# First attention group's norm, transposes, query and key moved into the last two steps of the text layers

## The chip, the cores and the metric

The kernel runs on one core of a Trainium2 chip. The metric is the device time of one execution in microseconds (us); the time of a kernel is the median over its runs. The engines are TensorE (PE), VectorE (DVE), ScalarE (ACT), GpSimd (POOL) and the DMA queues, of which SyncE (SP) issues most.

## What is computed

The model joins an image and a text, runs one attention layer over both and one layer of experts. Cut to what matters:

```python
h = concat([tokens_of_patches(x), text(x_txt)], axis=1)   # 32 sequences of 37 + 77 = 114 rows of 256
h = h + attention(layernorm(h))
h = h + experts(layernorm(h))

def text(tokens):                     # four layers
    xp = x @ W_in.T;  x_in, gate = split(xp)
    u = silu(causal_conv4(x_in) + cb)
    hs = scan(u @ WB.T)               # h = 0.95 h + 0.05 bu along the sequence
    y = (hs @ WC.T + Dv * u) * silu(gate)
    x = layernorm(y @ Wo.T + x) * g + b

def attention(x):
    qk = silu(x @ wqk + bqk);  q = qk*gamma0 + beta0;  k = qk*gamma1 + beta1
    v = silu(x @ wv + bv)
    a = causal(0.5*(1 + erf(...(q @ k.T / S + rel_bias))))
    return a @ v
```

The experts are eight, of which each row goes to two: the rows are scattered to tables by expert, and 64 blocks of 128 rows are worked through.

## The kernel before

The program has five instruction streams, one per engine, each written out by hand; semaphores alone order the engines among each other, and each engine works strictly in the order of its own stream. That order is the subject here.

**Text layers.** The 32 sequences stand in 8 groups of 4 (308 columns). A text step is one group of one layer, so there are 32 steps, 0 to 31 (`STEPS` is 32). They are pipelined: in iteration i the functions `text_step(i, a, b, o, t)` of the engines work on steps a = i, b = i-1, o = i-2 and t = i-3, and a part whose step does not exist is left out. Iterations 32, 33 and 34 therefore only drain steps 29 to 31. Step 31 ends so: PE multiplies `u` by W_B (L1241, L1249), DVE scans it (`scan`, L1689), ACT takes the upper half of the scanned state (`upper_state`, L773) and DVE the lower (`lower_state`, L1694), PE multiplies by W_C (`state_out`, L1261 and L1262, four chunks), DVE adds and gates (`skip` L1675, `gated` L1683), ACT and POOL split y into two halves (`upper_half` L766, `lower_half` L1026), PE adds the residual (L1273) and multiplies by W_out (L1278), DVE and POOL normalise (`row_stats`, `row_scale` L1019 and L1021, `row_norm` L1723), and POOL applies gain and shift (`keep_gain` L1050, `keep_rows` L1058). POOL's `text_step` runs one iteration ahead of the others in its numbering: its `lower_half(b, ...)` of iteration 31 waits for what ACT does in iterations 32 and 33.

**Between text and attention.** When the rows of a group are kept, SP stores them to memory (L617). After each pair of groups it waits for the stores and loads finished sequences, image and text rows together, into `h_all` (L625), group by group, `ld_h` counting them. The first four groups are loaded during the text layers, the last four after the last store.

**Attention.** 8 groups again, pipelined over 13 iterations of `attn_step(i)` on each engine. For a group g the parts are, in the order of their dependence:

- `norm_ahead_stats` (DVE, L1798 and L1801), `norm_ahead` (POOL, L1094 and L1096: variance plus epsilon, then power -0.5 into `a_rs`), `norm_bias` (DVE, L1812: minus mean times `a_rs`, into `a_nb`; two small operands in SBUF), `norm_rows` (ACT, L852, four instructions);
- `turn_rows` (PE, L1391, eight transposes), `rows_turned` (ACT, L859, two copies out of PSUM), `query_key` (PE, L1398), `query_key_silu`, `query`, `key` (ACT, L865, L870, L873);
- `bias_scores`, `values`, `scores` (PE, L1373, L1403 with L1406, L1381), `gate_values` (ACT, L884), `scale_scores`, `invert`, `weigh` (DVE, L1817, L1823, L1828), `attended` (PE, L1418);
- then the norm, the router and the sending of rows for the experts (L1428 to L1114), for which DVE first waits in `routed_stats` until all text rows are stored (L1839 is the copy just ahead) and until POOL has cleared `padbuf` (L1121, one memset after the last `keep_rows`).

Before the change DVE computes the first group's statistics in text iteration 32 and POOL their power in iteration 33, between `keep_gain(31)` and `keep_rows(31)`. Everything else of the attention, from `norm_bias(0)` on, stands after the last text iteration.

**Experts and the end.** After the last group a table of blocks is built, SP loads the blocks, PE runs them, and a last stage gathers, normalises and stores the result.

## Time and profile before

| | us |
|---|---|
| median of 3 runs | 1171.47 |
| lowest, highest run | 1166.38, 1176.45 |
| span of the profiled execution | 1176.4 |
| PE busy in it | 1024.7 (87%) |
| DVE busy | 718.6 (61%) |
| POOL busy | 599.9 (51%) |
| ACT busy | 578.8 (49%) |

The profiled execution's span, 1176.4 us, agrees with the highest of the three runs (1176.45), so hardly anything lies around it. The text layers fill the span up to about 553 us, the attention reaches to about 720, and the first expert block starts on PE at about 739. A timeline row gives start, duration, engine, line, operation, the buffers written and read, how many instructions were merged, and in brackets how long the engine sat idle before and what released it. Starts and durations of PE rows overlap, since matmuls are pipelined. The granted clock is a share of 2.4 GHz; 0.50 is 1.2 GHz.

### The profile page before, as it was taken

Reading aid. Unit: us, or ns where it says so; the run is one execution under the profiler, and the core shown is the slowest. Engines: PE = TensorE matmul, PEld = TensorE weight load, DVE = VectorE, ACT = ScalarE, POOL = GpSimd, SP = SyncE. Lnnn points to the kernel's source line nnn. Section 1 sums busy time; section 2 is a strip of 40 time slices with the busy share of each in tenths; the row PEclk is TensorE's granted clock in tenths of the full one; section 3 lists DMA queues with packets and bytes.
Section 4 is the critical chain, followed back from the end, with each engine's and each line's share of the span. In section 5 each row is a group of like instructions: output and inputs, shape, how many; then the busy total and the mean of one; then the engine's idle time right before and its main releaser. Section 6 shows DMA issues by size and latency. Waiting matters only on the chain.

```text
span 1176.4 us, 19799 instructions
## 1 busy us (share of the span) xinstructions
PE 1024.7 (87%) x5646; PEld 821.8 (70%) x5647; DVE 718.6 (61%) x1864; ACT 578.8 (49%) x1273; POOL 599.9 (51%) x662
## 2 busy tenths in 40 slices
PE   5888999999999999995888972899999999999920
PEld 4678999999999999994666652466666666666610
DVE  1667999999999988995466563233333333333337
ACT  1466777877787777662658551122222222222223
POOL 4534666676667767777136557133333333333336
PEclk8999999999999999997879785899999999999965
DMA  9460001000100000111635523122222222222263
GB/s 274 118 188 10 1 13 52 1 1 5 60 1 1 24 2 10 55 54 35 215 121 173 155 58 110 32 45 45 43 46 41 45 45 45 45 45 44 41 145 123
DMA packets 54732, 75.47 MB, mean 64 GB/s; under 512 B 9348, under 2 KB 46978, under 8 KB 52612
## 3 DMA queue, kind: packets, MB, share of 16 engines
q1 hardware_dynamic: 32680, 49.24, 13.6%
q0 software_dynamic: 16640, 18.53, 9.5%
q10 hardware_dynamic: 5340, 6.83, 2.1%
q8 instruction: 35, 0.57, 0.2%
q14 instruction: 37, 0.30, 0.1%
HBM read 45.38 MB, written 29.14 MB: 63 GB/s over the span
## 4 chain that ended last, share of the span: by engine, by line
PE 71%; DVE 9%; DMA 5%; POOL 5%; issue 4%; ACT 4%; SPq 1%; POOLq 0%; ACTq 0%; DVEq 0%
PE bank L1495 19%; PE bank L1213 15%; PE bank L1511 9%; PE bank L1278 7%; PE bank L1273 3%; PE bank L1406 3%; PE bank L1503 2%; PE bank L1418 2%; DMA xtok<-in_tok_emb,tokens_s 2%; PE bank L1261 2%; SPq L515 1%; PE bank L1262 1%; POOL xtok L994 1%; PE bank L1486 1%; DVE arena_b L1667 1%
## 5 line engine op out<-in xcount | busy, mean ns | idle before, releaser
L1141 POOL DMA_INDIRECT yrows<-arena_b,dest_i x64 | 99.7, 1557 | 272.6 <-ACT arena_b L953 261.6
L1495 PE MATMUL bank<-arena_a,arena_b 128*128 x512 | 236.0, 604 | 0.8 <-ACT arena_b L941 0.6
L1667 DVE SCALAR_TENSOR_TENSOR arena_b<-bank,sml,arena_b 128x304 f32<-128x304 f32 (+2 forms) x384 | 195.3, 522 | 19.7 <-ACT arena_b L742 16.9
L1975 DVE TENSOR_TENSOR arena_b<-bank,arena_b 128x512 f32<-128x512 f32 x64 | 44.3, 692 | 202.3 <-PE bank L1495 202.3
L1213 PE MATMUL bank<-xt_hi,w_hi 128*128 128x308 f32 x512 | 159.7, 312 | 4.6 <-DVE arena_b L1667 3.2
L1495 PEld LDWEIGHTS bank<-arena_a,arena_b 128*128 128x128 f32 x512 | 93.1, 192 | 98.7 <-issue 95.1
L1213 PE MATMUL bank<-xt_hi,w_lo 128*128 128x308 f32 x512 | 157.1, 307 | 0.0
L1213 PE MATMUL bank<-xt_lo,w_hi 128*128 128x308 f32 x512 | 156.7, 306 | 0.0
L1032 POOL TENSOR_TENSOR u_halves<-arena_b,u_halves 128x308 fp32r<-128x308 f32 x128 | 109.6, 863 | 28.3 <-ACT arena_b L754 28.2
L1511 PE MATMUL bank<-arena_a,arena_b 128*128 x512 | 122.6, 382 | 1.1 <-DVE arena_b L1991 0.9
L1026 POOL TENSOR_TENSOR y_lo<-arena_b,y_hi 128x308 fp32r<-128x308 f32 x128 | 107.7, 855 | 26.8 <-ACT y_hi L766 26.6
L1213 PEld LDWEIGHTS bank<-xt_hi,w_hi 128*128 128x128 f32 x512 | 97.9, 191 | 5.4 <-DVE arena_b L1667 3.5
L1511 PEld LDWEIGHTS bank<-arena_a,arena_b 128*128 128x128 f32 x512 | 92.3, 190 | 13.4 <-issue 2.7
L1213 PEld LDWEIGHTS bank<-xt_hi,w_lo 128*128 128x128 f32 x512 | 97.9, 191 | 0.0
L1213 PEld LDWEIGHTS bank<-xt_lo,w_hi 128*128 128x128 f32 x512 | 97.5, 191 | 0.0
L947 ACT ACTIVATE arena_b<-bank 128x512 f32<-128x512 f32 x64 | 38.2, 598 | 114.0 <-PE bank L1495 114.0
L1114 POOL DMA_INDIRECT xrows<-arena_b,slot_i x64 | 73.1, 1142 | 26.2 <-issue 17.2
L742 ACT ACTIVATE arena_b<-bank,sml 128x308 f32<-128x308 f32 x128 | 76.9, 602 | 17.6 <-PE bank L1213 12.2
L1278 PE MATMUL bank<-w_hi,y_hi 128*128 128x256 f32 (+1 forms) x320 | 81.4, 281 | 0.0
L1278 PE MATMUL bank<-w_lo,y_hi 128*128 128x256 f32 (+1 forms) x320 | 81.2, 281 | 0.0
L1675 DVE SCALAR_TENSOR_TENSOR bank<-arena_b,sml,bank 128x308 f32<-128x308 f32 x128 | 68.1, 534 | 18.1 <-PE bank L1262 18.0
L953 ACT ACTIVATE arena_b<-bank,row_wt 128x256 f32<-128x256 f32 x64 | 30.4, 475 | 95.5 <-PE bank L1511 87.3
(193 smaller groups left out, 2230.9 us busy)
## 6 DMA issues: line engine op xcount, KB each, us to landing
arena_b<-xrows SPq DMA_DIRECT2D x64, 129.5 KB, 2.1
arena_a<-in_w_gate SPq DMA_DIRECT2D x4, 1024.0 KB, 9.4
arena_a<-in_w_up SPq DMA_DIRECT2D x4, 1024.0 KB, 6.9
arena_a<-in_w_down SPq DMA_DIRECT2D x4, 1024.0 KB, 7.9
yrows<-arena_b SPq DMA_DIRECT2D x1, 3648.0 KB, 18.7
h_all<-seq SPq DMA_DIRECT2D x8, 448.0 KB
w_raw<-in_w_in SPq DMA_DIRECT2D x3, 1024.0 KB, 4.7
arena_a<-yrows SPq DMA_DIRECT2D x4, 448.0 KB
```

The costliest lines, as they stand in the source:

```text
L742: act.activation(u[s % 2][:, c, :], x_bank(c)[:, 0:GT], ACT.Identity, bias=SML(W_CB + s // GROUPS * FC + c), scale=conv_w(s // GROUPS, c, ...
L1026: pool.tensor_tensor(y_half(y_lo, s, c), y_full[:, c, :], y_half(y_hi, s, c).bitcast(F32), ALU.subtract)\
L1032: pool.tensor_tensor(u_halves[s % 2][:, 1, c, :], u[s % 2][:, c, :], u_halves[s % 2][:, 0, c, :].bitcast(F32), ALU.subtract).then_inc(pool ...
L1114: pool.indirect_dma_start(xrows, bass.IndirectOffsetOnAxis(ap=to, axis=0), a_x[g % ROW_SETS][:, b, :], None).then_inc(x_sent[g % ROW_SETS] ...
L1141: pool.indirect_dma_start(yrows, bass.IndirectOffsetOnAxis(ap=dest_i[:, k:k + 1], axis=0), f_y[k], None, compute_op=ALU.add).then_inc(y_se ...
L1213: mm = pe.matmul(out_, in_half(w, layer, d, slice(c * P, (c + 1) * P)), x[:, d, cols], start=(k == 0), stop=(k == len(pairs) - 1))
L1278: return pe.matmul(out_tile(j), y[:, c, PAIR_AT[j]:PAIR_AT[j] + PAIR_ROWS[j]], out_half(w, s // GROUPS, c), start=False, stop=stop, skip_g ...
L1495: mm = pe.matmul(bank[q][:, :], x_gt[k][:, d, :], w[:, d, bass.ds(e * FFN, FFN)], start=(d == 0), stop=(d == DC - 1))
L1511: mm = pe.matmul(bank[4 + k][:, 0:D], f_ht[k][:, c, :], wd_s[:, c, bass.ds(e * D, D)], start=(c == 0), stop=(c == FC - 1))
L1667: dve.scalar_tensor_tensor(acc[:, :, back_:TXT], x[:, :, 0:TXT - back_], conv_w(s // GROUPS, c, tap), acc[:, :, back_:TXT], ALU.mult, ALU. ...
L1675: dve.scalar_tensor_tensor(y1, u[s % 2][:, c, :], SML(W_D + s // GROUPS * FC + c), y1, ALU.mult, ALU.add)\
L1975: dve.tensor_tensor(f_h, bank[1][:, :], f_sg, ALU.mult).then_inc(f_hh, 1)
```

## The change

The functions `norm_rows`, `rows_turned`, `query_key_silu`, `query`, `key` and the others of ACT's attention, and those of PE's, are defined ahead of `text_step` and are otherwise unchanged. The parts of group 0 up to the silu of query and key are called from the text steps, `norm_ahead_stats(1)`, `norm_ahead(1)` and `norm_bias(1)` too, the memset of `padbuf` moves behind `norm_ahead(2)`, and all `attn_step` loops start at 2.

```diff
 # ACT, text_step
                 if live(t):
                     upper_half(t, 3)
+                if i == STEPS + 1:
+                    norm_rows(0)
+                if i == STEPS + 2:
+                    query_key_silu(0)
...
                 if live(a):
                     conv_start(a, 0)
+                if i == STEPS + 1:
+                    rows_turned(0, 0)
                 if live(o):
                     upper_half(o, 0)
+                if i == STEPS + 1:
+                    rows_turned(0, 1)
 # ACT, attn_step
-                if has(i - 2):
+                if has(i - 2) and i > 2:
                     rows_turned(i - 2, 0)
                     rows_turned(i - 2, 1)
...
-                if has(i - 2):
+                if has(i - 2) and i > 2:
                     query_key_silu(i - 2)
...
-                if has(i - 1):
+                if has(i - 1) and i > 1:
                     norm_rows(i - 1)
...
-            for i in range(GROUPS + LAST_LAG):
+            for i in range(2, GROUPS + LAST_LAG):
                 attn_step(i)
 # POOL, text_step
                 if live(b):
                     lower_half(b, 1)
-                if i == STEPS + 1:
+                if i == STEPS - 1:
                     norm_ahead(0)
                 if live(b):
                     lower_half(b, 2)
                     lower_half(b, 3)
                 if live(o) and not turns(o):
                     keep_rows(o)
+                if i == STEPS:
+                    norm_ahead(1)
...
             pool.wait_ge(rows_kept, GROUPS)
-            pool.memset(padbuf[:, :, :], 0.0).then_inc(pad_zero, 1)
 
             def attn_step(i):
...
-                if has(i) and i:
+                if has(i):
                     norm_ahead(i)
+                if i == 2:
+                    pool.memset(padbuf[:, :, :], 0.0).then_inc(pad_zero, 1)
 # PE, text_step
                 if live(o):
                     state_out(o, 0)
                     state_out(o, 1)
+                if i == STEPS + 1:
+                    turn_rows(0, 0)
+                    turn_rows(0, 1)
...
                 if live(o):
                     residual(o)
+                if i == STEPS + 1:
+                    pe.wait_ge(ld_qkv, 32)
+                    query_key(0)
...
 # PE, attn_step
-                if has(i - 3):
+                if has(i - 3) and i > 3:
                     query_key(i - 3)
...
-                if has(i - 2):
+                if has(i - 2) and i > 2:
                     turn_rows(i - 2, 0)
                 if has(i - 5):
                     ranks(i - 5)
+                if has(i - 2) and i > 2:
+                    turn_rows(i - 2, 1)
                 if has(i - 2):
-                    turn_rows(i - 2, 1)
                     bias_scores(i - 2)
 # DVE, text_step
                 if live(o):
                     lower_state(o)
+                if i == STEPS + 2:
+                    norm_ahead_stats(1)
                 if live(t):
                     row_stats(t)
                     row_moments(t)
+                if i == STEPS + 2:
+                    norm_bias(1)
...
+                if i == STEPS:
+                    norm_bias(0)
                 if live(b):
                     scan(b)
```

**The order on POOL, iteration 31.** The rows are one piece of POOL's stream around the last two y halves of step 30. `y_lo` is `lower_half`, `w_raw` as an operand marks `keep_gain` and `keep_rows`, `a_rs` is `norm_ahead`. Before:

```order
L1032 TENSOR_TENSOR u_halves<-arena_b,u_halves 128x308
L1026 TENSOR_TENSOR y_lo<-arena_b,y_hi 128x308
L1032 TENSOR_TENSOR u_halves<-arena_b,u_halves 128x308
L1026 TENSOR_TENSOR y_lo<-arena_b,y_hi 128x308 x3
L1058 TENSOR_TENSOR arena_b<-arena_b,w_raw 128x768
L1019 TENSOR_SCALAR arena_b<-arena_b 128x3
```

The same place after the change (lines are those of the changed file):

```order
L1040 TENSOR_TENSOR u_halves<-arena_b,u_halves 128x308
L1034 TENSOR_TENSOR y_lo<-arena_b,y_hi 128x308
L1104 TENSOR_SCALAR a_rs<-a_mv 114x4
L1106 TENSOR_TENSOR a_rs<-a_rs,minus_half 114x4
L1034 TENSOR_TENSOR y_lo<-arena_b,y_hi 128x308 x2
L1066 TENSOR_TENSOR arena_b<-arena_b,w_raw 128x768
L1027 TENSOR_SCALAR arena_b<-arena_b 128x3
```

`norm_ahead(0)` came in between `lower_half(30, 1)` and `lower_half(30, 2)`; two halves and `keep_rows(29)` stand right behind it.

**The order on DVE and ACT, iterations 32 and 33.** DVE after the change, from the last gating of step 30 to the lower state of step 31 (`hs_halves`); the line without `a_nb` in it is the order before:

```order
L1692 SCALAR_TENSOR_TENSOR bank<-arena_b,sml,bank 128x308
L1700 TENSOR_TENSOR arena_b<-bank,arena_b 128x308
L1835 SCALAR_TENSOR_TENSOR a_nb<-a_mv,a_rs 114x4
L1706 SCALAR_TENSOR_TENSOR bank<-arena_b,bank 128x308
L1711 TENSOR_TENSOR hs_halves<-bank,hs_halves 64x308
```

ACT after the change, from `norm_rows(0)` to `query_key_silu(0)`; before, the rows with `hs_halves` and `y_hi` stand alone:

```order
L794 ACTIVATE arena_b<-h_all,a_nb,a_rs 114x256 x4
L773 ACTIVATE hs_halves<-bank 128x308
L773 ACTIVATE hs_halves<-bank 64x308
L801 ACTIVATE arena_b<-bank 128x456
L766 ACTIVATE y_hi<-arena_b 128x308
L801 ACTIVATE arena_b<-bank 128x456
L766 ACTIVATE y_hi<-arena_b 128x308 x3
L804 ACTIVATE warm<-minus_half 1x1
```

`norm_bias(0)` now stands in front of `scan(31)` on DVE, and `norm_rows(0)` in front of `upper_state(31)` on ACT.

**The order on PE, from the last residual to the attention.** Before, behind the last product of the text layers (`w_hi,y_lo`):

```order
L1278 MATMUL bank<-w_hi,y_lo 128x256 x2
L1278 MATMUL bank<-w_hi,y_lo 104x256
L1391 MATMUL bank<-cst,arena_b 128x114 x8
L1373 MATMUL bank<-bias_h,ident_a 114x456 x2
L1398 MATMUL bank<-arena_b,arena_a 128x456 x2
L1403 MATMUL bank<-bv_rows,bv_ones 114x512
L1406 MATMUL bank<-arena_a,arena_b 114x256 x4
```

After the change, at the same place:

```order
L1289 MATMUL bank<-w_hi,y_lo 128x256 x2
L1289 MATMUL bank<-w_hi,y_lo 104x256
L1322 MATMUL bank<-bias_h,ident_a 114x456 x2
L1352 MATMUL bank<-bv_rows,bv_ones 114x512
L1355 MATMUL bank<-arena_a,arena_b 114x256 x4
```

The eight transposes moved up between the second and third `state_out` of step 31, and `query_key(0)` between its residual and `out_upper(31, 0)`.

## Rows read from the trace of the kernel before

**Rows 1.** The waits, 522 to 600 us: who waited for whom, total, times, longest.

```profile
PE bank L1391 <- ACT arena_b L852: 11.1, 1, 11.1
```

**Rows 2.** PE's timeline, end of the text layers and start of the attention.

```profile
538.02 0.38 PE L1261 MATMUL bank<-hs_halves,wc_halves 128*128 128x308 f32 x1 [1.20 <-DVE arena_b L1683]
...
543.66 1.23 PE L1278 MATMUL bank<-w_hi,y_lo 128*128 128x256 f32 x9
556.00 1.75 PE L1391 MATMUL bank<-cst,arena_b 114*128 114x114 f32 x8 [11.11 <-ACT arena_b L852]
...
558.40 3.08 PE L1398 MATMUL bank<-arena_b,arena_a 128*128 128x456 f32 x4
561.40 0.48 PE L1403 MATMUL bank<-bv_rows,bv_ones 33*114 33x512 f32 x1
```

**Rows 3.** PE's timeline, second group's transposes, bias, query and key.

```profile
566.88 0.95 PE L1391 MATMUL bank<-cst,arena_b 114*128 114x114 f32 x8
567.59 0.65 PE L1373 MATMUL bank<-bias_h,ident_a 114*114 114x456 f32 x2
568.51 1.80 PE L1398 MATMUL bank<-arena_b,arena_a 128*128 128x456 f32 x4 [0.28 <-ACT arena_b L859]
```

**Rows 4.** POOL's timeline, 530 to 554 us.

```profile
530.62 1.65 POOL L1026 TENSOR_TENSOR y_lo<-arena_b,y_hi 128x308 fp32r<-128x308 f32 x2
532.57 0.84 POOL L1026 TENSOR_TENSOR y_lo<-arena_b,y_hi 128x308 fp32r<-128x308 f32 x1 [0.31 <-ACT y_hi L766]
533.38 1.54 POOL L1058 TENSOR_TENSOR arena_b<-arena_b,w_raw 128x768 f32<-128x768 f32 x1
...
550.86 0.23 POOL L1094 TENSOR_SCALAR a_rs<-a_mv 114x4 f32<-114x4 f32 x1
...
552.18 1.54 POOL L1058 TENSOR_TENSOR arena_b<-arena_b,w_raw 128x768 f32<-128x768 f32 x1
553.79 3.34 POOL L1121 MEMSET padbuf<- 128x3885 f32 x1
```

**Rows 5.** DVE's timeline: the scan of step 31 and the first norm bias.

```profile
533.85 0.80 DVE L1689 TENSOR_TENSOR_SCAN bank<-arena_b,bank 128x308 f32<-128x308 f32 x1 [1.85 <-PE bank L1249]
...
552.25 1.50 DVE L1812 SCALAR_TENSOR_TENSOR a_nb<-a_mv,a_rs 114x4 f32<-114x4 f32 x1 [3.24 <-POOL a_rs L1096]
```

**Rows 6.** DVE's timeline at two earlier text steps, one line, the same operation.

```profile
139.10 3.22 DVE L1614 TENSOR_TENSOR arena_b<-arena_b,tab_s 114x1216 f32<-114x1216 f32 x1
...
231.10 1.92 DVE L1614 TENSOR_TENSOR arena_b<-arena_b,tab_s 114x1216 f32<-114x1216 f32 x1
```

**Rows 7.** POOL's timeline beside them.

```profile
138.53 2.50 POOL L1026 TENSOR_TENSOR y_lo<-arena_b,y_hi 128x308 fp32r<-128x308 f32 x3
...
230.88 0.86 POOL L1026 TENSOR_TENSOR y_lo<-arena_b,y_hi 128x308 fp32r<-128x308 f32 x1 [0.76 <-ACT y_hi L766]
```

**Rows 8.** ACT's timeline at the end of the text layers.

```profile
534.69 0.73 ACT L773 ACTIVATE hs_halves<-bank 128x308 fp32r<-128x308 f32 x2 [2.19 <-DVE bank L1689]
...
553.78 2.07 ACT L852 ACTIVATE arena_b<-h_all,a_nb,a_rs 114x256 f32<-114x256 f32 x4 [10.99 <-DVE a_nb L1812]
```

**Rows 9.** Windows: us, busy time (count) of each engine, granted clock, DMA share, GB/s.

```profile
530.00:534.00 4.00, 3.83 (x17) 3.77 (x18) 1.57 (x5) 1.30 (x3) 3.69 (x5) 0.57 0.02 4
534.00:538.00 4.00, 2.50 (x19) 2.08 (x18) 3.01 (x8) 0.82 (x3) 1.81 (x3) 1.00 0.24 72
538.00:542.00 4.00, 3.98 (x29) 3.68 (x30) 3.39 (x8) 1.22 (x3) 2.89 (x4) 1.00 0.08 23
576.00:580.00 4.00, 4.00 (x12) 3.12 (x12) 1.97 (x11) 0.26 (x1) 1.26 (x2) 0.50 1.01 422
```

**Rows 10.** SP's timeline: first load of the last four groups.

```profile
558.34 12.77 SPq L625 DMA_DIRECT2D h_all<-seq  x8
```

**Rows 11.** DVE's timeline: first weighing of scores, first routed statistics.

```profile
570.48 0.63 DVE L1828 TENSOR_TENSOR arena_b<-arena_b,arena_a 114x456 f32<-114x456 f32 x1 [0.60 <-ACT arena_b L879]
...
575.96 0.17 DVE L1839 COPY padbuf<-cst 128x15 f32<-128x15 f32 x1
```

More of the change, by code:

```diff
@@ L909, in attn_step @@
+            act.wait_ge(zeroed, ZEROED)
+            text_iterations(text_step)
             def attn_step(i):
-                if has(i - 2):
+                if has(i - 2) and i > 2:
                     rows_turned(i - 2, 0)
@@ L1131, in attn_step @@
                     routed_scale(i - 2)
-            for i in range(GROUPS + LAST_LAG):
+            for i in range(2, GROUPS + LAST_LAG):
                 attn_step(i)
@@ L1466, in attn_step @@
                     ranks(i - 5)
+                if has(i - 2) and i > 2:
+                    turn_rows(i - 2, 1)
                 if has(i - 2):
-                    turn_rows(i - 2, 1)
                     bias_scores(i - 2)
-            for i in range(GROUPS + LAST_LAG):
+            for i in range(2, GROUPS + LAST_LAG):
                 attn_step(i)
@@ L1911, in attn_step @@
                     scale_scores(i - 2)
-                if has(i) and i:
+                if has(i):
                     norm_ahead_stats(i)
@@ L1927, in attn_step @@
                     routed_stats(i - 2)
-            for i in range(GROUPS + LAST_LAG):
+            for i in range(2, GROUPS + LAST_LAG):
                 attn_step(i)
```

221 lines of the change are left out of this document (109 added, 112 removed).

## Prediction

> **What bounds the kernel now.** I read the list of waits first, then the timelines of PE, POOL, DVE and ACT around the end of the text layers, then windows for the clock. The waits name one hole: PE waits 11.1 us for the first `norm_rows` [rows 1]. PE's timeline shows it whole: the last text product ends at 543.66 + 1.23 = 544.89, eight transposes start at 556.00, query and key at 558.40, and the first `values` at 561.40 [rows 2]. So 16.5 us pass between text and `values`, and all of it is the chain of the first group's norm, transposes, query and key. Nothing of that chain needs the last text group: its rows were loaded long before, and its power waits on POOL between `keep_gain(31)` and `keep_rows(31)`.
>
> From `values(0, 0)` on, each attention step follows from the one before it. I take an earlier start there as an earlier end, unless something that did not move comes last; I check that below.
>
> **What is taken away.** After the change PE goes from the last text product to `bias_scores(0)` and then to `values(0, 0)`. `bias_scores` takes 0.65 us at full clock [rows 3]. Saved: 561.40 - 544.89 - 0.65 = 15.85 us, if the text layers end when they did. They don't, for three reasons.
>
> **First cost: `norm_bias(0)` meets POOL, 3.35 us.** `norm_ahead(0)` now follows `lower_half(30, 1)`, which ends about 530.62 + 0.82 = 531.44 (half of a row of two) [rows 4]. It takes 552.18 - 550.86 = 1.32 us, so it ends near 532.76. At once behind it stand `lower_half(30, 2)`, `lower_half(30, 3)` and `keep_rows(29)`: 0.82 + 0.81 + 1.54 = 3.17 us without a gap, up to 535.93 [rows 4]. `norm_bias(0)` on DVE waits for the end of `norm_ahead(0)`, so it is issued as POOL starts that run. Exactly this pair stands in the trace: at 552.25 `norm_bias(0)` starts just after POOL's 552.18, and takes 1.50 us for four columns, to 553.75, where POOL's row ends at 553.72 [rows 4, 5]. Two earlier rows say how long DVE waits when POOL has several instructions in a row. At 231.10 a product of two SBUF operands ends at 233.02, 1.28 us after POOL's one instruction (231.74). At 139.10 the same operation ends at 142.32, 1.29 us after POOL's run of three (141.03), though two of the three started after it [rows 6, 7]. So DVE waited for the whole run, not for one instruction.
>
> The Trainium skill has the rule behind this, in "SBUF — State Buffer", section "Who interferes with whom": a DVE instruction with two SBUF inputs contends with a GpSimd instruction that reads SBUF, and the second to issue blocks until the first finishes. The rows agree on the block, but by that wording one instruction would be waited for, and the result would be the first rival's.
>
> Hence `norm_bias(0)` ends near 535.95. Two things are behind it. `scan(31)` stood at 533.85 [rows 5] and goes to 535.97. On ACT, `norm_rows(0)` takes 2.07 us, to 538.05, and `upper_state(31)`, which stood at 534.69, is queued behind it [rows 8]. So `state_out(31, 0)` on PE, and all that follows it, comes 3.35 us late. If DVE did not wait at all, ACT, idle for 2.19 us before 534.69, would run `norm_rows(0)` from 532.95 to 535.05, and the cost would be 0.35. These are the ends, 0.35 and 3.35; I take 3.35, for the row at 139.10.
>
> **Second cost: query and key, 1.8 us.** `query_key(0)` stands on PE between the residual and `out_upper(31, 0)`. In 538 to 542 PE was busy 3.98 of 4 us [rows 9], so nothing there hides it: 1.80 us at full clock [rows 3]. The eight transposes stand ahead of `state_out(31, 2)`, before which PE waited 1.20 us for DVE's gating [rows 2]; at 0.95 us [rows 3] they fit into that wait. Without that cover they would cost 0.95, and at the low clock they take 1.75 [rows 2], 0.55 more than the wait.
>
> **Third cost: the clock, 1.0 us.** PE would stand idle for over 3 us ahead of `state_out(31, 0)`. After its idle of 11.1 us the transposes ran slow, 1.75 us against 0.95 for the same eight later [rows 2, 3], that is at the lower level of 1.2 GHz. With 1.5 us idle out of 4, in 534 to 538, the granted clock was 1.00 [rows 9]. Over 3 us lies between, nearer to the second, but in 530 to 534 the clock was 0.57 although PE was busy 3.83 of 4 us [rows 9], so it does fall in this part of the text. If only the two `state_out` and the transposes run slow, about 0.8 us comes on top (0.23 for the first, 0.55 for the second). If residual and query and key run slow too, it is 0.8 + 1.5 + 1.28 = 3.6 (the residual's 1.5 us is estimated from its twelve products between the rows of 538.02 and 543.66; 1.28 is 3.08 - 1.80 [rows 2, 3]). Below nothing it can't go, since PE ran at full clock there. I take 1.0, since the clock of 534 to 538 was back at 1.00 right after the slow window.
>
> **What costs nothing.** `rows_turned` on ACT and `query_key_silu`, `query`, `key` lie beside PE's residual and last products; if that cover went, `scores(0)` would wait, and `values(0, 0)`, which needs none of them, would still run. `norm_ahead_stats(1)` and `norm_ahead(1)` (1.32 us) stand where DVE and POOL wait for PE's last product; uncovered, they would cost 1.32. `norm_bias(1)` may be held by POOL's `row_scale(31)`, but `row_norm` behind it waits for that anyway. `norm_ahead(0)` leaves the space between `keep_gain(31)` and `keep_rows(31)`, so the rows are kept at 553.72 + 6.15 - 1.32 = 558.55. SP's first load of the last groups followed by 558.34 - 553.72 = 4.6 us [rows 4, 10], so the text is stored by 563.2. The first routed statistics, at 575.96 before [rows 11], would want it at 566.3: 3.1 us of cover.
>
> The memset of `padbuf`, 3.34 us [rows 4], moves behind `norm_ahead(2)`: 558.55 + 1.32 = 559.87, to 563.2. In it falls `weigh(0)`, two SBUF operands, at 570.48 - 9.7 = 560.8 [rows 11]. No row shows such an instruction beside a memset. If it were held, up to 2.4 us would be lost; at the other end nothing. I take 0, because every hold in rows 4 to 7 was beside a POOL instruction that reads two operands, and keep 2.4 for the range. The skill's page says the same in that section: an instruction that only writes is no rival for the port; by this the sum would stay as it is.
>
> **The sum.** -15.85 + 3.35 + 1.80 + 1.0 = -9.7 us. Against the profiled execution (1176.4, the highest of the three runs) that is 1166.7; it stands 4.9 us above the median. Against the median 1171.47 - 9.7 = 1161.8. With the bounds above (clock 0 to 3.6, memset 0 to 2.4) the forecast's own range is -10.7 to -4.7: 1160.8 to 1166.8.
>
> **Rivals.**
>
> *The hold is short.* If DVE waits for one POOL instruction, `norm_bias(0)` ends at 532.76 + 0.82 = 533.6, `norm_rows(0)` at 535.7, and `upper_state(31)` is 1.0 late; the wait of PE stays near the 1.2 us at which the clock was kept [rows 2, 9]. Gain 15.85 - 1.0 - 1.8 = 13.05: 1158.4. If it doesn't wait at all, 15.85 - 0.35 - 1.8 = 13.7: 1157.8. For it: the row at 552.25 was followed by a memset, so it shows one instruction only [rows 4, 5]. Against it: the row at 139.10 [rows 6, 7]. Chance 0.25.
>
> *The gain is absorbed.* Something that did not move ends last, and the attention's end stays: about 1171. For it: the last text rows are stored later than before, by 5 us, and the routed part waits for them. Against it: 3.1 us of cover, and the sending at the end of the attention hangs on the last group alone. Chance 0.09.
>
> *Slower: PE stays at 1.2 GHz.* After the new idle PE restarts low and stays so up to the second group's query and key. Then the text's last work (538.02 to 544.89, 6.87 us) and `values` and `scores` of the first group (561.40 to 566.88, 5.48) take as long again, and to it come 0.65 for the bias, 1.28 each for two times query and key, 0.55 and 0.80 for the transposes: 16.9 us against 15.85 - 3.35 - 1.8 = 10.7. The kernel would be 6.2 slower: 1177.7. It decides from 10.7 us of such work on, some 1.3 us into the first `values`. For it: in 576 to 580 PE was busy all the time, and the clock was 0.50 [rows 9]. Against it: the clock of 534 to 542. Chance 0.06.
>
> The forecast keeps 0.60.
>
> **How the numbers follow.** The three runs lie up to 5 us from their median, and a measurement can tell about 1%, 11.7 us, from no change; the bound for faster is 1159.8. The forecast lies 2 us short of it and falls beyond in one case of five (0.12); the short hold falls beyond in seven of ten (0.18). Faster 0.30. Slower by over 1% would need the slow rival and more: 0.02. The rest, 0.68, is within 1%. The range takes in the short hold with some of the runs' spread below, 1155, and goes up to 1170, which leaves out the slow rival and half of the absorbed case.
>
> **What would show it.** Right: `norm_bias(0)` on DVE near 3 us long, ending with POOL's `keep_rows(29)`; `upper_state(31)` about 3.4 us after its old place; PE's last text product ending near 551; `values(0, 0)` 0.7 us after it, some 9.7 us earlier than 561.40; the same shift at the first expert block. Wrong: a `norm_bias(0)` under 1 us (first rival); a shift of 9.7 at `values` that is gone at the experts (second); a granted clock of 0.50 through 540 to 555 (third); and a `weigh(0)` that ends with the memset, for the term taken as 0.

## Result and profile after

| | before | after |
|---|---|---|
| median us, first comparison (4 runs each) | 1173.74 | 1159.69 |
| lowest, highest | 1166.38, 1176.45 | 1156.18, 1165.86 |
| ratio of the runs, in brackets its 95% interval | | 0.9892 [0.9858, 0.9926] |
| span of the profiled execution | 1176.4 | 1160.9 |

The changed kernel was run in two more comparisons: 1160.37 (6 runs, ratio 0.9886 [0.9861, 0.9911]) and 1163.59 (6 runs, 0.9916 [0.9887, 0.9944]). Over all its 16 runs the mean is 1161.3, that of 33 runs of before 1173.2, a gain of 11.9 us, 95% interval 10.1 to 13.7 (10.3 between the medians 1162.48 and 1172.74). The forecast was a gain of 9.7 and 1161.8 us, its first rival's 13.05 and 1158.4.

PE's timeline, which answers to [rows 2] and [rows 3] (line numbers of the changed file: L1272 is `state_out`, L1340 `turn_rows`, L1347 `query_key`, L1289 the text product, L1322 `bias_scores`, L1352 `values`, L1367 `attended`):

```profile
536.03 0.60 PE L1272 MATMUL bank<-hs_halves,wc_halves 128*128 128x308 f32 x1 [2.00 <-ACT hs_halves L773]
...
537.19 1.72 PE L1340 MATMUL bank<-cst,arena_b 114*128 114x114 f32 x8
...
541.81 1.91 PE L1347 MATMUL bank<-arena_b,arena_a 128*128 128x456 f32 x4
...
547.16 1.23 PE L1289 MATMUL bank<-w_hi,y_lo 128*128 128x256 f32 x9
548.23 0.58 PE L1322 MATMUL bank<-bias_h,ident_a 114*114 114x456 f32 x2
548.74 0.49 PE L1352 MATMUL bank<-bv_rows,bv_ones 33*114 33x512 f32 x1
...
554.11 0.94 PE L1340 MATMUL bank<-cst,arena_b 114*128 114x114 f32 x8
```

The wait of 11.1 us [rows 1] is gone. The text ends at 547.16 + 1.23 = 548.39, and `values(0, 0)` follows 0.35 us later, where 16.51 passed before. The last step of the text has become longer: state_out(31, 0) to the end takes 548.39 - 536.03 = 12.36 us, 8.86 before. A new wait of 2.00 us for `upper_state(31)` stands just ahead of it. Everything before this stretch ran 0.94 us earlier than in the first profile (state_out(30, 3) at 529.23 against 530.17), so from here on 0.94 is taken off where the two profiles are compared by the clock on the wall.

The first cost lies on POOL, DVE and ACT, answering to [rows 4], [rows 5] with the first of [rows 11], and [rows 8]. POOL:

```profile
530.82 1.04 POOL L1106 TENSOR_TENSOR a_rs<-a_rs,minus_half 114x4 f32<-114x4 f32 x1
531.83 1.65 POOL L1034 TENSOR_TENSOR y_lo<-arena_b,y_hi 128x308 fp32r<-128x308 f32 x2
533.43 1.54 POOL L1066 TENSOR_TENSOR arena_b<-arena_b,w_raw 128x768 f32<-128x768 f32 x1
...
557.43 3.34 POOL L1138 MEMSET padbuf<- 128x3885 f32 x1
```

DVE:

```profile
531.89 0.80 DVE L1835 SCALAR_TENSOR_TENSOR a_nb<-a_mv,a_rs 114x4 f32<-114x4 f32 x1 [1.04 <-POOL a_rs L1106]
532.61 0.79 DVE L1706 TENSOR_TENSOR_SCAN bank<-arena_b,bank 128x308 f32<-128x308 f32 x1
...
557.51 0.16 DVE L1835 SCALAR_TENSOR_TENSOR a_nb<-a_mv,a_rs 114x4 f32<-114x4 f32 x1
557.71 0.63 DVE L1851 TENSOR_TENSOR arena_b<-arena_b,arena_a 114x456 f32<-114x456 f32 x1
...
562.93 0.17 DVE L1862 COPY padbuf<-cst 128x15 f32<-128x15 f32 x1
```

ACT:

```profile
532.73 2.08 ACT L794 ACTIVATE arena_b<-h_all,a_nb,a_rs 114x256 f32<-114x256 f32 x4 [1.39 <-DVE a_nb L1835]
534.71 0.71 ACT L773 ACTIVATE hs_halves<-bank 128x308 fp32r<-128x308 f32 x2
```

`norm_bias(0)` (L1835) ends at 532.69. POOL's pair behind the power gives a first end at 531.83 + 1.65 / 2 = 532.66; its run ends at 534.97. So DVE was held for one instruction, not for the run. The scan starts at once, but `upper_state(31)` (L773) has to wait on ACT for the end of `norm_rows(0)`, 1.3 us after the scan's end at 533.40. And `weigh(0)` (L1851) takes 0.63 us in the midst of the memset: no hold there.

The windows, answering to [rows 9]:

```profile
530.00:534.00 4.00, 3.70 (x27) 3.13 (x25) 2.33 (x4) 1.74 (x4) 3.92 (x6) 1.00 0.02 4
...
536.00:538.00 2.00, 1.97 (x9) 1.97 (x10) 1.94 (x6) 0.00 (x0) 0.89 (x2) 0.50 0.41 119
538.00:540.00 2.00, 2.00 (x11) 2.00 (x10) 1.74 (x4) 1.34 (x3) 0.89 (x2) 0.50 0.17 50
540.00:542.00 2.00, 2.00 (x11) 2.00 (x11) 0.91 (x3) 0.85 (x2) 2.00 (x3) 0.50 0.00 0
542.00:544.00 2.00, 2.00 (x9) 1.16 (x8) 0.00 (x0) 0.00 (x0) 1.01 (x2) 0.94 0.00 0
```

PE was at 1.2 GHz from 536 to about 542 and at 2.4 GHz in 530 to 534, just the other way round than before [rows 9]. SP's load, answering to [rows 10]:

```profile
560.66 12.81 SPq L625 DMA_DIRECT2D h_all<-seq  x8
```

The last texts are stored by 560.66, and the routed part wants them at 562.93 (L1862, the second of [rows 11]): covered by 2.3 us.

### The profile page after: what moved, and what is told of

Same layout as the page of the kernel before. It is cut to its first block, busy times and chain, and to the rows that moved or that the text cites. A ratio compares the mean times of both kernels' runs of the same rounds, so it can differ in the third digit from the quotient of the medians.

```text
span 1160.9 us, 19799 instructions
## 1 busy us (share of the span) xinstructions
PE 1019.3 (88%) x5646; PEld 818.8 (71%) x5647; DVE 714.1 (62%) x1864; ACT 578.9 (50%) x1273; POOL 601.2 (52%) x662
## 3 DMA queue, kind: packets, MB, share of 16 engines
q1 hardware_dynamic: 32680, 49.24, 13.5%
## 4 chain that ended last, share of the span: by engine, by line
PE 71%; DVE 7%; POOL 5%; DMA 5%; ACT 5%; issue 5%; SPq 2%; POOLq 0%; ACTq 0%; DVEq 0%
PE bank L1512 19%; PE bank L1224 15%; PE bank L1528 9%; PE bank L1289 7%; PE bank L1284 3%; PE bank L1520 2%; PE bank L1355 2%; PE bank L1367 2%; DMA xtok<-in_tok_emb,tokens_s 2%; PE bank L1272 2%; PE bank L1273 1%; SPq L515 1%; POOL xtok L1002 1%; PE bank L1503 1%; DVE arena_b L1684 1%
## 5 line engine op out<-in xcount | busy, mean ns | idle before, releaser
L1528 PEld LDWEIGHTS bank<-arena_a,arena_b 128*128 128x128 f32 x512 | 92.3, 190 | 12.8 <-issue 2.8
L1289 PE MATMUL bank<-w_hi,y_hi 128*128 128x256 f32 (+1 forms) x320 | 81.4, 282 | 0.0
L1289 PE MATMUL bank<-w_lo,y_hi 128*128 128x256 f32 (+1 forms) x320 | 80.9, 280 | 0.0
```

The lines of the kernel that those rows point to most:

```text
L1289: return pe.matmul(out_tile(j), y[:, c, PAIR_AT[j]:PAIR_AT[j] + PAIR_ROWS[j]], out_half(w, s // GROUPS, c), start=False, stop=stop, skip_g ...
L1528: mm = pe.matmul(bank[4 + k][:, 0:D], f_ht[k][:, c, :], wd_s[:, c, bass.ds(e * D, D)], start=(c == 0), stop=(c == FC - 1))
```

## The experiments

Twelve experiments, e1 to e12, in three comparisons. The table gives, from each profile, what passes from the start of `scan(31)` to state_out(31, 0), from there to the end of the last text product, and from there to `values(0, 0)`; it is worked out from rows like those above.

| kernel | to state_out | to text end | to values | sum | median us (runs) |
|---|---|---|---|---|---|
| before | 2.18 | 8.86 | 16.51 | 27.55 | 1173.74 (4) |
| before again (e8) | 2.18 | 8.84 | 16.85 | 27.87 | 1173.38 (1) |
| after | 3.42 | 12.36 | 0.35 | 16.13 | 1159.69 (4) |
| after again (e1) | 3.23 | 10.19 | 0.34 | 13.76 | 1160.37 (6) |
| after again (e9) | 3.41 | 11.67 | 0.34 | 15.42 | 1163.59 (6) |
| norm behind state (e2) | 2.18 | 10.29 | 0.35 | 12.82 | 1157.36 (6) |
| the same (e10) | 2.18 | 10.30 | 0.35 | 12.83 | 1157.26 (5) |
| norm alone (e3) | 2.16 | 8.95 | 3.19 | 14.30 | 1160.14 (7) |
| query and key behind text (e4) | 3.41 | 8.85 | 1.89 | 14.15 | 1162.18 (6) |
| power behind rows (e5) | 3.42 | 12.42 | 0.35 | 16.19 | 1161.94 (4) |
| second group behind text (e6) | 3.42 | 12.37 | 0.34 | 16.13 | 1165.60 (4) |
| small probes (e7) | 3.42 | 10.19 | 0.35 | 13.96 | 1158.69 (1) |
| transposes ahead (e11) | 3.41 | 10.20 | 0.34 | 13.95 | 1159.91 (6) |
| norm behind both (e12) | 2.18 | 10.29 | 0.34 | 12.81 | 1159.48 (6) |

**The changed kernel again (e1).** No edit.

> The changed kernel once more. Theory: the hold of norm_bias(0) by POOL can end at any boundary between two POOL instructions, and which one is chance; then norm_bias(0) takes 0.8 us again or 1.6 or about 3.1, and scan(31) and norm_rows(0) follow it. Rival: it ends at the first boundary always, 0.80 us to within 0.05. For the 2.65 us that came between attended(0) and attended(1): if it follows from the change, the two start 15.2 us apart again; if it was chance, 17.8 us as before the change can come back. Ratio to the kernel before 0.985 to 0.993.

Its windows and PE's row of state_out(31, 0):

```profile
530.00:534.00 4.00, 3.82 (x18) 3.78 (x19) 2.50 (x6) 1.63 (x4) 3.92 (x6) 0.59 0.01 4
...
536.00:538.00 2.00, 1.02 (x8) 1.05 (x9) 1.56 (x6) 0.37 (x2) 0.03 (x1) 1.00 0.24 70
538.00:540.00 2.00, 1.59 (x14) 1.41 (x13) 1.58 (x4) 1.45 (x3) 1.09 (x2) 1.00 0.40 118
```

```profile
536.98 0.38 PE L1272 MATMUL bank<-hs_halves,wc_halves 128*128 128x308 f32 x1 [1.38 <-ACT hs_halves L773]
```

The same program, and this time the low clock lies in 530 to 534, as before the change; the text's end runs at full clock and takes 2.17 us less. So the clock's cost there belongs to the execution, not to the program: 2.17 in the first profile, 0 in this, 1.48 in e9. `norm_bias(0)` took 0.80 us again, as the rival said. And the first two `attended` start 17.84 us apart here, 15.19 in the first profile after the change: that step, too, is the execution's.

**`norm_rows(0)` behind `upper_state(31)` (e2, and e10 with more runs).**

```diff
 # ACT, text_step
-                if i == STEPS + 1:
-                    norm_rows(0)
...
                     upper_state(o, 1)
+                if i == STEPS + 1:
+                    norm_rows(0)
```

> The changed kernel with norm_rows(0) on ACT behind upper_state(31) in place of ahead of it. Theory: norm_rows(0) ahead of upper_state(31) made state_out(31, 0) 0.94 us late, and the idle of 2.0 us on PE that came of it brought the low clock; then state_out(31, 0) comes 1.0 us earlier against scan(31), the idle is about 1.0, the clock in the residual is 1.00, and from state_out(31, 0) to the end of the last text product it takes 10.7 to 11.5 us in place of 12.4; values(0, 0) 2 to 2.7 us earlier against the text. Rival: the transposes and not the idle bring the clock down, or PE had slack; then it takes 12.4 us again and values(0, 0) gains 1.0 at most.

> norm_rows(0) stands behind upper_state(31) on ACT, the same kernel as the second experiment. Theory of the path (what stands ahead of upper_state(31) delays the rest by its length, some 1 us here, and a shorter wait of PE keeps the clock more often): 1 to 3 us faster than the changed kernel in the same rounds, ratio 0.984 to 0.988. Rival (the difference of the first medians, 3 us, was the spread of single executions): within 1 us of the changed kernel.

ACT's timeline of e2:

```profile
533.61 0.73 ACT L773 ACTIVATE hs_halves<-bank 128x308 fp32r<-128x308 f32 x2 [1.95 <-DVE bank L1706]
534.24 2.07 ACT L794 ACTIVATE arena_b<-h_all,a_nb,a_rs 114x256 f32<-114x256 f32 x4
```

From scan to state_out the kernel is back at the 2.18 us of before: 1.24 of the first cost is `norm_rows(0)` in front of `upper_state(31)`. The ratios are 0.9876 [0.985, 0.9902] and 0.9875 [0.9847, 0.9903]. Over its 11 runs the mean is 3.8 us below that of the changed kernel's 16 (95% interval 1.4 to 6.1, from drawing the runs anew; 2.3 and 6.0 in the two comparisons), more than the 2.3 us between the sums of the table (12.8 against a mean of 15.1 for the three). The table doesn't show where the rest is from. This version beats both kernels. PE's wait ahead of state_out(31, 0) is 0.35 us and the text's end 10.29, less than expected. But the low stretch lay ahead of it (0.71 in 530 to 534; in e10 0.62 in 526 to 530), as in e1, where the changed kernel takes 10.19. So these runs don't show that the shorter wait kept the clock up.

**The norm alone early (e3).** `turn_rows`, `rows_turned`, `query_key` and its silu of group 0 go back behind the text, `norm_rows(0)` stands as in e2.

```diff
 # PE, text_step
-                    turn_rows(0, 0)
-                    turn_rows(0, 1)
...
-                    query_key(0)
 # PE, attn_step
-                if has(i - 3) and i > 3:
+                if has(i - 3):
                     query_key(i - 3)
...
```

> Only the norm of the first group is early (power on POOL, bias on DVE, norm_rows(0) on ACT behind upper_state(31)); transposes, their copies, query and key stand behind the text layers as before the change. Theory: nearly all of the gain comes from the norm chain and none from having PE's part in the text layers, since PE has to do transposes, query and key either way; text ends as before the change (8.9 us from state_out(31, 0) to the last product), values(0, 0) starts 3.4 to 3.8 us after the last product (0.95 transposes, 0.65 bias, 1.8 query and key, copies of ACT beside them), and the sum over both is at most 0.5 us longer than the changed kernel's 12.4 + 0.35, or up to 1 us shorter because the clock stays up. Rival: PE's part is hidden in the text layers; then this kernel is 2.5 to 4 us slower than the changed one.

Ratio 0.9874 [0.9853, 0.9896]. Without the norm to wait for, transposes, bias, query and key take 3.19 us behind the text (3.4 to 3.8 expected), and the text's end is 8.95, as before. The norm's place alone brings as much as the whole change: the mean of these runs is 1160.0 us, of the changed kernel's 1161.3. But this kernel also has the place of `norm_rows(0)` from e2, so PE's part has to be measured against e2. There, moving it gives 3.19 - 0.35 = 2.84 and costs 10.29 - 8.95 = 1.34, a gain of 1.5 us in PE's rows. The runs can't tell: the mean here is 2.5 us above that of e2 and e10 (95% interval -0.1 to 5.5).

**Query and key behind the text (e4).**

```diff
 # PE, text_step
-                if i == STEPS + 1:
-                    pe.wait_ge(ld_qkv, 32)
-                    query_key(0)
...
+            pe.wait_ge(ld_qkv, 32)
             pe.wait_ge(bias_seq, BIAS_OPS)
...
 # PE, attn_step
-                if has(i - 3) and i > 3:
+                if has(i - 3):
                     query_key(i - 3)
```

> The changed kernel with query_key(0) on PE behind the last text product, all else as changed. Theory: query and key cost PE 1.8 us wherever they stand, as PE has no idle there; the text ends 1.8 us earlier, values(0, 0) starts 2.4 us after the last product, and the time of values(0, 0) is the same to within 0.3 us. Rival: query_key(0) in the text layers was hidden by a wait; then values(0, 0) comes 1.8 us later than in the changed kernel.

Ratio 0.99 [0.9874, 0.9927]. Against e1 the text's end is 1.34 us shorter and the gap 1.55 longer: query and key cost nearly the same in either place. The eight transposes, still in the text here, cost nothing (8.85 against 8.86): the wait ahead of state_out(31, 2) hides them.

**The first power behind POOL's run (e5).** The place at which a hold for the whole run would have put it.

```diff
 # POOL, text_step
-                if i == STEPS - 1:
-                    norm_ahead(0)
...
                     keep_rows(o)
+                if i == STEPS - 1:
+                    norm_ahead(0)
```

> The first group's power stands on POOL behind keep_rows(29) instead of between lower_half(30, 1) and lower_half(30, 2): the place at which a hold of norm_bias(0) for POOL's whole run would have put it. Theory of the path (what stands in front of scan(31) and of upper_state(31) moves state_out(31, 0), and the rest follows): norm_bias(0) can start only some 3.2 us later than in the changed kernel (0.82 + 0.81 + 1.54 us of POOL's work now stand in front), so state_out(31, 0) starts about 3.3 us later than before instead of 0.9, PE runs part of the text end at the lower clock, and values(0, 0) comes 2 to 5 us after the changed kernel's; kernel 2 to 5 us slower than the changed one, ratio to the kernel before about 0.991 to 0.994. Rival (the end of the text has slack on this chain): state_out(31, 0) late, but text end and values(0, 0) as in the changed kernel within 0.5 us, ratio 0.987 to 0.989.

PE:

```profile
537.36 0.60 PE L1272 MATMUL bank<-hs_halves,wc_halves 128*128 128x308 f32 x1 [5.40 <-ACT hs_halves L773]
```

DVE:

```profile
533.86 0.16 DVE L1835 SCALAR_TENSOR_TENSOR a_nb<-a_mv,a_rs 114x4 f32<-114x4 f32 x1 [4.28 <-POOL a_rs L1106]
```

With POOL at rest `norm_bias(0)` takes 0.16 us. The scan comes 5.62 us after PE starts `state_in(31)`, against 2.9 to 3.0 in the changed kernel, and `values(0, 0)` 21.81 after it, against 16.7 to 19.2: the price of the forecast's first cost, as expected. The time doesn't show it: ratio 0.9896 [0.9857, 0.9934], the mean of 4 runs 0.3 us above the changed kernel's (-3.3 to 3.9). That part of the expectation is open.

**The second group's norm behind the text (e6).** `norm_ahead_stats(1)`, `norm_ahead(1)` and `norm_bias(1)` leave the text steps.

```diff
 # DVE and POOL, behind the text steps
...
-            for i in range(2, GROUPS + LAST_LAG):
+            for i in range(1, GROUPS + LAST_LAG):
                 attn_step(i)
```

> The second group's statistics, power and bias go back behind the text layers, where they stood before; the first group's parts stay early. Theory of cover (they cost nothing in the text and their early place is needed, since DVE and POOL are late there): norm_ahead(1) then stands on POOL behind keep_rows(31), norm_rows(1) on ACT waits for it, and the second group's transposes on PE come 3 to 6 us later than in the changed kernel; values(1, 0) late by as much, kernel 3 to 5 us slower than the changed one, ratio 0.991 to 0.993. Rival (PE has other work there, values and scores of the first group, and the second group is hidden behind it): values(1, 0) within 0.5 us of the changed kernel's, ratio 0.987 to 0.989.

```profile
559.21 1.78 PE L1338 MATMUL bank<-cst,arena_b 114*128 114x114 f32 x8 [5.57 <-ACT arena_b L794]
```

PE's wait for a norm is back, for the second group now: 5.57 us (none in the changed kernel, 554.11 above), and the transposes behind it take 1.78 in place of 0.94. `values(1, 0)` comes 20.1 us after `values(0, 0)`, against 13.5 to 13.8 in the changed kernel, a little more than expected. Ratio 0.9922 [0.9899, 0.9945], mean 4.0 us above the changed kernel (2.1 to 5.9). That part of the change is needed.

**Small probes (e7).** A product of four columns into a scratch, 26 times:

```diff
 # DVE
+        probe = sb("probe", [SEQ, 104])
...
 # DVE, text_step
+                if 6 <= i < STEPS:
+                    dve.scalar_tensor_tensor(probe[:, (i - 6) * 4:(i - 6) * 4 + 4], cst[0:SEQ, 0:8:2], -1.0,
+                                             cst[0:SEQ, C_CAUSAL:C_CAUSAL + 4], ALU.mult, ALU.mult)
```

> The changed kernel plus, in each of the text iterations 6 to 31, one four-column product of two SBUF operands on DVE into a scratch of its own, like norm_bias(0). It meets POOL in the middle of different runs of instructions. Theory of size (a small instruction gets in as soon as POOL's present instruction ends): every one takes at most some 1.7 us and ends with the end of one POOL instruction, none ends with the second or third of a run. Theory of chance (which boundary lets DVE in is open, as for the wide products of the causal table): some end with one instruction and some with a whole run of two or three, 2 to 3.3 us. Theory of no port (such an instruction isn't held at all, 0.80 us was something else): all take about 0.15 us, also where POOL is busy all the time.

Two of them on DVE, and POOL beside them:

```profile
377.17 1.95 DVE L1806 SCALAR_TENSOR_TENSOR probe<-cst 114x4 f32<-114x4 f32 x1
...
479.08 0.66 DVE L1806 SCALAR_TENSOR_TENSOR probe<-cst 114x4 f32<-114x4 f32 x1
```

```profile
376.61 2.49 POOL L1035 TENSOR_TENSOR y_lo<-arena_b,y_hi 128x308 fp32r<-128x308 f32 x3
...
477.07 2.64 POOL L1035 TENSOR_TENSOR y_lo<-arena_b,y_hi 128x308 fp32r<-128x308 f32 x3 [0.20 <-ACT y_hi L767]
479.68 1.54 POOL L1067 TENSOR_TENSOR arena_b<-arena_b,w_raw 128x768 f32<-128x768 f32 x1
```

All 26 were held; none took 0.15 us. Nine met a POOL instruction that had another right behind it. Six of them got in at its end, like 479.08, which ends at 479.74 as `keep_rows` starts. Three were passed over, like 377.17, which ends at 379.12 with POOL's run of three (379.10). How late in POOL's instruction they were issued goes with it. The five with 0.6 us or more of it left got in, all of them; of the four with 0.13 to 0.30 left three were passed over (POOL's ends inside a merged row are estimated by equal parts). Four of the five early ones had `keep_rows` behind, so these nine alone don't part the moment of issue from what follows; `norm_bias(0)`, also early, had a y half behind. The theory of chance holds, for late issues.

**The kernel before, again (e8).** No edit.

> The kernel before, unchanged, for a second profile. Theory that the attention's steps have two lengths by the clock in each execution, whatever the kernel: the step from the first to the second attended is again 15.2 or 16.8 or 17.8 to 19.2 us, some other step differs by 1.5 to 2.7 us from the first profile's, and the sum from values(0, 0) to the first expert block (177.3 us) moves by up to some 7 us. Rival (the steps are set by the change): each of the seven steps within 0.2 us of the first profile's 17.83, 18.27, 19.69, 16.81, 18.41, 19.58, 15.52.

Two rows of PE's first two `attended`:

```profile
572.09 1.95 PE L1418 MATMUL bank<-arena_b 114*114 114x256 f32 x8 [2.79 <-ACT arena_b L884]
...
587.28 3.16 PE L1418 MATMUL bank<-arena_b 114*114 114x256 f32 x8 [2.12 <-issue]
```

The step is 15.19 us here; in the first profile of before it was 17.83. From `values(0, 0)` to the first expert block it is 173.86 us against 177.30. As theory said, the attention's length is the execution's. In the text, PE had the full clock where the first profile had the lower one (0.57 in 530 to 534 [rows 9]). This matters for the first cost below.

```profile
530.00:534.00 4.00, 3.64 (x29) 3.65 (x30) 2.42 (x5) 1.95 (x5) 3.91 (x5) 1.00 0.02 4
```

**Transposes ahead of state_out(31, 0) (e11).**

```diff
 # PE, text_step
+                if i == STEPS + 1:
+                    turn_rows(0, 0)
+                    turn_rows(0, 1)
                 if live(o):
                     state_out(o, 0)
                     state_out(o, 1)
-                if i == STEPS + 1:
-                    turn_rows(0, 0)
-                    turn_rows(0, 1)
```

> The eight transposes of the first group stand on PE ahead of state_out(31, 0) instead of behind state_out(31, 1), in the wait for upper_state(31). Theory of the idle (PE's clock falls in the text end because PE waits 1.4 to 2 us for upper_state(31) right behind a stretch at the lower level; work in that wait keeps it up): state_out(31, 0) starts no later than in the changed kernel, the residual and query and key run at full clock (query and key 1.7 us), 10.2 us from state_out(31, 0) less 0.5 for the transposes to the end of the text. Rival (the clock there comes from what lies earlier, not from this wait): as often at the lower level as the changed kernel, and the wait for the gating of chunk 2 takes the time of the transposes. Either way the kernel is within 2 us of the changed one.

```profile
536.88 0.38 PE L1272 MATMUL bank<-hs_halves,wc_halves 128*128 128x308 f32 x1 [1.18 <-DVE arena_b L1700]
```

The wait for the gating is back at 1.18 us, as the rival said, and the end of the text is 10.20. But in this profile the low clock lay ahead (0.68 in 530 to 534), as in e1, so it doesn't tell whether filling the wait keeps the clock. Ratio 0.9894 [0.9867, 0.9921], the mean 0.7 us below the changed kernel's 16 runs (-1.9 to 3.2). Inconclusive.

**`norm_bias(0)` behind `scan(31)` too (e12).**

```diff
 # DVE, text_step, on top of the edit of e2
-                if i == STEPS:
-                    norm_bias(0)
                 if live(b):
                     scan(b)
+                if i == STEPS:
+                    norm_bias(0)
```

> As the second experiment, and norm_bias(0) stands behind scan(31) on DVE too: nothing of the first group's norm is left ahead of step 31's last chain. Theory of the path: scan(31) starts when PE's product for it ends, state_out(31, 0) 2.2 us after the scan's start as in the kernel before, so up to 0.7 us earlier than in the second experiment, and the kernel is 1 to 3 us faster than the changed one, ratio 0.983 to 0.988. norm_bias(0) is held by POOL or not, and nothing waits for it but norm_rows(0). Rival (norm_rows(0) then comes so late that the transposes stand in front of state_out(31, 2) without cover): state_out(31, 2) late by up to 1 us, and the kernel no faster than the second experiment's.

```profile
532.91 0.80 DVE L1706 TENSOR_TENSOR_SCAN bank<-arena_b,bank 128x308 f32<-128x308 f32 x1 [1.83 <-PE bank L1260]
533.62 0.15 DVE L1835 SCALAR_TENSOR_TENSOR a_nb<-a_mv,a_rs 114x4 f32<-114x4 f32 x1
```

```profile
532.05 1.64 POOL L1034 TENSOR_TENSOR y_lo<-arena_b,y_hi 128x308 fp32r<-128x308 f32 x2
533.65 1.55 POOL L1066 TENSOR_TENSOR arena_b<-arena_b,w_raw 128x768 f32<-128x768 f32 x1
```

Nothing stands in front of the scan, and yet it comes no earlier than in e2, 3.08 us after PE's `state_in(31)` against 2.90: PE, at the low clock here, released it. In e8, at full clock, PE released it 1.80 us after `state_in(31)`, so this profile doesn't show what the place is worth at full clock. `norm_bias(0)` was issued 0.07 us before the end of POOL's second y half (533.69) and got in ahead of `keep_rows(29)`, in 0.15 us. Ratio 0.9889 [0.9861, 0.9917], the mean 2.0 us below the changed kernel's 16 runs (-0.6 to 4.4); not shown to be better than e2 or than the changed one. The changed kernel itself in that comparison (e9):

> The changed kernel itself once more, as the measure for the three beside it. Both theories expect 1158 to 1163 us and a ratio of 0.985 to 0.992 to the kernel before. From state_out(31, 0) to the end of the text PE takes 12.4 us when the granted clock falls there, or 10.2 when it doesn't.

Its median, 1163.59 us, lies just above what was expected, and its text end, 11.67, between the two values: the first two state_out and the transposes ran at full clock, and the low stretch came from 540 on (0.50 in 540 to 542).

## Why the prediction was right, and where not

**The frame held.** One wait stood between text and attention, and its removal is the gain. Saved: 16.51 - 0.35 = 16.16 us, forecast 15.85; the difference is the bias, 0.34 apart in PE's starts rather than 0.65.

**The first cost was the step that failed:** "So DVE waited for the whole run, not for one instruction", 3.35 us. In all ten profiles in which it follows the power at this place, `norm_bias(0)` took 0.80 or 0.81 us, held for one instruction: under 1 us, the sign that the prediction had named for its first rival. Between the first two profiles state_out(31, 0) came 536.03 - 536.03 + 0.94 = 0.94 us late; the first rival had said 1.0. The row that I leaned on [rows 6, 7] was no model. It was issued at 139.10, some 0.26 us before the end of POOL's first instruction, late in it. `norm_bias(0)` follows POOL's power and so always meets the next instruction at its start, with 0.77 us of it left. Even that row is only the commoner of two outcomes: over the fourteen profiles the same product takes 3.2 us in ten and some 1.57 in four, though it is issued 0.55 to 0.60 us after the start of POOL's first instruction in all of them. What decides there stays open. In the profile after it is the short one, on DVE:

```profile
139.78 1.58 DVE L1631 TENSOR_TENSOR arena_b<-arena_b,tab_s 114x1216 f32<-114x1216 f32 x1
```

The other two rows of [rows 4 to 7] were issued early in an instruction with nothing like it behind and could not tell. The Trainium skill, "SBUF — State Buffer", section "Summary: rules for kernel authors", says that the second to issue blocks until the first finishes. For `norm_bias(0)` and for 23 of the 26 probes the traces agree with that wording; for the three probes passed over it is too short, and the measurement decides.

The 0.94 is a sum of three things, and one of them is not the change's. `norm_rows(0)` in front of `upper_state(31)` costs 1.24 (3.42 - 2.18, and e2 gives them back). `norm_bias(0)` in front of `scan(31)` costs 1.2: PE's product for the scan ended at 530.63 + 0.73 = 531.36, and the scan started at 532.61, as `norm_bias(0)` ended. Against them stand 1.5 us of the clock: that product ran at full clock in this execution, and at the lower one in the first profile of before (530 to 534: 1.00, there 0.57). The second profile of before (e8) had full clock there too. PE after the change, and DVE in e8:

```profile
530.63 0.73 PE L1260 MATMUL bank<-u_halves,wb_halves 128*64 128x308 f32 x4
```

```profile
532.52 0.80 DVE L1689 TENSOR_TENSOR_SCAN bank<-arena_b,bank 128x308 f32<-128x308 f32 x1 [0.55 <-PE bank L1249]
```

The starts of state_out(30, 3) and state_out(31, 0), in the first profile of before, in e8, and the first of them after the change (the second is 536.03, shown above):

```profile
530.17 0.49 PE L1261 MATMUL bank<-hs_halves,wc_halves 128*128 128x308 f32 x1 [2.26 <-DVE arena_b L1683]
...
536.03 0.38 PE L1261 MATMUL bank<-hs_halves,wc_halves 128*128 128x308 f32 x1 [0.33 <-issue]
```

```profile
530.36 0.38 PE L1261 MATMUL bank<-hs_halves,wc_halves 128*128 128x308 f32 x1 [2.27 <-DVE arena_b L1683]
...
534.70 0.38 PE L1261 MATMUL bank<-hs_halves,wc_halves 128*128 128x308 f32 x1 [0.34 <-issue]
```

```profile
529.23 0.38 PE L1272 MATMUL bank<-hs_halves,wc_halves 128*128 128x308 f32 x1 [2.27 <-DVE arena_b L1700]
```

From the first to the second the two profiles of before take 5.86 us (lower clock) and 4.34 (full clock), the three of the changed kernel 6.79 or 6.80, at either clock. So the first cost was 0.94 where PE had the lower clock there (e1 against the first profile of before) and 2.46 where it had the full one (after against e8), 1.7 on average. The forecast had read the scan's old place, 533.85 [rows 5], from a stretch at the lower clock.

**The second cost** was 1.8 and measured 1.34 (e1 against e4). That the transposes fit into the wait for the gating was right (e4).

**The third cost** was 1.0, with bounds 0 to 3.6: it was 2.17, 0 and 1.48 in three profiles of the changed kernel, 1.2 on average. The reason given for it, the new idle of PE, is not shown. In the changed kernel the low clock came after the wait of 2.00 us where PE had been at full clock ahead of it, and not where a low stretch lay just ahead (e1, 1.38 us idle). But e4 has the same wait behind a full clock (1.00 in 530 to 534), and its text end ran at full clock:

```profile
537.54 0.38 PE L1272 MATMUL bank<-hs_halves,wc_halves 128*128 128x308 f32 x1 [2.00 <-ACT hs_halves L773]
```

What decides it stays open.

**The sum.** In the first pair of profiles: -16.16 + 0.94 + (12.36 - 8.86) = -11.72, and PE's rows give 561.40 - 0.94 - 548.74 = 11.72. The spans differ by 15.5: 0.94 lies ahead of it, and 177.30 - 174.03 = 3.27 behind, in the attention, which e8 shows to be no work of the change; what comes after took 0.4 longer. (Every run's time on record lies 1.8 to 3.1 us above the span of its core. So the first profile of before, with its span of 1176.4, is not the run of 1176.45 that the text ahead takes it for, but a longer one.) Over both profiles of before and all three of the changed kernel the terms are -16.34 saved, 1.70 for the first cost, 1.34 for the second and 1.22 for the clock: -12.1, near the 11.9 of the means. Of the 2.4 us that the forecast's 9.7 falls short, the first cost is 1.65, the wait and query and key are 0.5 each, and the clock goes 0.2 the other way. That the time was met in spite of it was luck in the sizes: 2.4 us is less than the spread of the runs. The hold is the first rival's, to which the forecast gave a chance of 0.25, and its gain of 13.05 is the nearer one.

**What was taken as nothing.** The memset does not hold `weigh(0)`: 0.63 us, as before [rows 11]. Nor does it hold `norm_bias(2)`, which is issued just after the memset starts: 0.16 us at 557.51, where `norm_bias(0)` of before, just after the start of `keep_rows(31)`, took 1.50 [rows 5]. The stored texts were covered, by 2.3 us (3.1 forecast). `norm_ahead(1)` in the text cost nothing and is needed (e6). **The other rivals** fell: the shift at `values` is still there at the first expert block (738.70 before, 722.77 after), so nothing absorbed it, and PE was at full clock again from 544 on, so it did not stay low.

## What to carry to other kernels

When a small chain waits for a norm, move the norm first: that alone brought as much as the whole change here, and moving PE's part as well 1.5 us in PE's rows. Put what is brought forward behind the urgent instruction of each queue, not in front of it: one place further back on ACT gave another 2 to 4 us. Before a row is taken as a model of a hold, look at where in the other engine's instruction it was issued, and at the same row in a second profile. Before two profiles are compared, look at the clock in the stretch: the same delay reads as 0.94 or 2.46 us, as PE had the lower or the full clock there.

## What was not expected of the hardware

A DVE instruction with two SBUF operands that was issued with 0.6 us or more of POOL's present instruction left got in at its end in every case: five probes, and `norm_bias(0)` in ten profiles. Issued in the last 0.3 us, it was passed over in three cases of five (four probes, and `norm_bias(0)` in e12), and then waited for the rest of POOL's run; the wide product of [rows 6] in ten of fourteen. What decides between them isn't shown. And the attention's 174 us vary by some 8 us between executions whatever the kernel: 170.8 to 178.5 from `values(0, 0)` to the first expert block over fourteen profiles. The same stretch of before in its two profiles, first and e8, shows the granted clock beside it:

```profile
572.00:580.00 8.00, 6.90 (x20) 4.78 (x21) 3.31 (x12) 2.54 (x5) 1.26 (x2) 0.67 0.94 327
```

```profile
572.00:580.00 8.00, 7.91 (x41) 6.14 (x42) 5.10 (x17) 4.86 (x10) 1.27 (x2) 1.00 0.95 318
```

At 0.67 PE did 20 products in 6.90 us, at 1.00 41 in 7.91; eight products of `values` in this stretch take 3.76 us in the first profile and 1.98 in e8. So the attention alone spreads over 7.8 us, a large part of the spread of the runs, and this is the reason why differences of 1 to 3 us between these kernels are read from stretches of the trace and not from the medians.
